# Two self-attentions: the product of exponentials and inverse sums is split by rows between VectorE and Pool

## What is computed

```
# third block (no mask)                     # fifth block (causal, q and k rotated)
scores = einsum('bhqd,bhkd->bhqk', q, k) / sqrt(dh)
attn = softmax(scores, axis=-1)
ctx = einsum('bhqk,bhkd->bhqd', attn, v)
out = ctx.reshape(B, S, D) @ wo.T + bo
```

## Time and profile before

| what | value |
|---|---|
| median of 3 runs | 3099.32 us (3094.27 to 3100.01) |
| the profiled execution | 3100.76 us, its span 3098.9 us |
| mean granted TensorE clock | 0.956 |
| busy share of the span | PE 92%, DVE 42%, ACT 31%, POOL 9% |
| stage 3's attention, scores to last output copy | 1026.4 to 1069.3 us of the span |
| stage 5's attention, scores to last output copy | 2855.5 to 2892.7 us of the span |

### The profile page before, as it was taken

The page is one execution under the profiler, slowest core; times in us unless marked ns, Lnnn a source line. Parts: engine busy times, 40 slices in busy tenths (PEclk is TensorE's granted clock), DMA queues, the critical chain, the costliest instruction groups (busy, mean ns, idle before and its releaser), DMA issues.

```text
span 3098.9 us, 36175 instructions
## 1 busy us (share of the span) xinstructions
PE 2852.6 (92%) x15608; PEld 1977.8 (64%) x15608; DVE 1305.4 (42%) x1978; ACT 973.3 (31%) x1471; POOL 263.6 (9%) x271
## 2 busy tenths in 40 slices
PE   7877989888898889999999969999999999997798
PEld 3335447356584468888888848878877877853432
DVE  4355374467731433333333342443343344354511
ACT  3233223124440344343334412332332332331300
POOL 1110110112000000000000011011001101000000
PEclk9988999998899989999999979999999999998799
DMA  8872794961021032222222210100100100012098
GB/s 354 314 280 97 303 375 164 359 236 65 14 82 68 30 111 102 99 95 95 96 95 95 97 70 21 45 21 25 45 25 21 45 25 21 25 62 95 29 414 358
DMA packets 63487, 385.23 MB, mean 124 GB/s; under 512 B 6193, under 2 KB 12593, under 8 KB 33889
## 3 DMA queue, kind: packets, MB, share of 16 engines
q1 hardware_dynamic: 27072, 190.58, 16.4%
q0 software_dynamic: 29776, 188.15, 15.8%
q10 hardware_dynamic: 6480, 4.20, 0.4%
HBM read 377.64 MB, written 5.26 MB: 124 GB/s over the span
## 4 chain that ended last, share of the span: by engine, by line
PE 76%; DVE 9%; DMA 7%; ACT 5%; issue 2%; POOL 1%; SPq 0%; DVEq 0%; POOLq 0%; ACTq 0%
PE PS L427 10%; PE PS L429 10%; PE PS L428 10%; PE PS L306 4%; PE PS L1707 4%; PE PS L614 4%; PE PS L1688 3%; PE PS L1671 3%; PE PS L1689 3%; PE PS L1690 3%; PE PS L1673 3%; PE PS L1672 3%; DMA ring<-in_experts 3%; PE PS L587 3%; PE PS L1724 2%; DMA PR<-in_ctxN 2%
## 5 line engine op out<-in xcount | busy, mean ns | idle before, releaser
L427 PE MATMUL PS<-X_high,W_high 128*128 128x512 f32 x576 | 226.4, 393 | 11.0 <-DVE X_low L1160 11.0
L427 PE MATMUL PS<-H_high,W_high 128*128 128x512 f32 x576 | 224.9, 390 | 2.1 <-DVE rstd L1461 2.1
L428 PE MATMUL PS<-X_low,W_high 128*128 128x512 f32 x576 | 225.8, 392 | 0.0
L429 PE MATMUL PS<-X_high,W_part 128*128 128x512 f32 x576 | 225.7, 392 | 0.0
L1107 DVE TENSOR_TENSOR W_part<-ring,W_high 128x2048 fp32r<-128x2048 f32 x63 | 147.0, 2334 | 185.0 <-ACT W_high L1103 185.0
L429 PE MATMUL PS<-H_high,W_part 128*128 128x512 f32 x576 | 224.7, 390 | 0.0
L428 PE MATMUL PS<-H_low,W_high 128*128 128x512 f32 x576 | 224.7, 390 | 0.0
L1103 ACT ACTIVATE W_high<-ring 128x2048 fp32r<-128x2048 f32 x72 | 137.0, 1915 | 252.4 <-PE PS L429 252.4
L1871 DVE TENSOR_TENSOR RB<-PS,rows 128x512 f32<-128x512 f32 x104 | 71.9, 691 | 306.8 <-PE PS L1690 306.8
L1146 DVE TENSOR_TENSOR H_low<-T,H_high 128x512 fp32r<-128x512 f32 x144 | 99.4, 690 | 210.5 <-ACT H_high L1133 210.4
L1671 PE MATMUL PS<-C_high,W_part 128*128 128x384 f32 (+2 forms) x512 | 177.3, 346 | 4.9 <-DVE W_part L1843 4.9
(11 more groups left out here) (336 smaller groups left out, 5571.8 us busy)
## 6 DMA issues: line engine op xcount, KB each, us to landing
ring<-in_experts SPq DMA_DIRECT2D x96, 1024.0 KB, 4.9
ring<-in_tiles SPq DMA_DIRECT2D x39, 1024.0 KB, 4.9
RC<-in_ctxN POOLq DMA_DIRECT2D x24, 1536.0 KB, 11.7
RA<-in_ctxT POOLq DMA_DIRECT2D x20, 1536.0 KB, 7.1
T<-in_ctxN POOLq DMA_DIRECT2D x24, 1024.0 KB, 14.3
RA<-in_experts SPq DMA_DIRECT2D x24, 1024.0 KB, 12.6
RA<-in_ctxT POOLq DMA_DIRECT2D x12, 1666.0 KB, 13.4
RB<-in_ctxT POOLq DMA_DIRECT2D x12, 1666.0 KB, 16.7
```

Source lines behind the costliest of these rows:

```text
L427: pe.matmul(ps, a, xh, start=start, stop=False)
L428: pe.matmul(ps, a, xl, start=False, stop=False)
L429: return pe.matmul(ps, b, xh, start=False, stop=stop)
```

## The change

Block bp's product for the rows 64 to 127 (u = 1) goes from DVE to Pool. DVE keeps the one for the rows 0 to 63 (u = 0). The shape, the operands and the output of each instruction stay as they are. Pool waits for its own instructions before, for DVE's reciprocal (which now has a name, `inverse{bp}`), and for the transposes of block bp - 2 or the zeros. PE's transposes wait for both products, and so does DVE's maxima(bp + 2), since it writes the `raw5` that both have read.

```diff
+        def attn_products(eng, at, tag, bp, u):
+
+            x, sm, r = raw5[bp % 2], sums[bp % 2], slice(u * S, (u + 1) * S)
+            if bp >= 2:
+                eng.wait_ge(*at.done(f"{tag}.T{bp - 2}.3"))
+            else:
+                eng.wait_ge(*at.done(f"{tag}.zero{bp}"))
+            eng.tensor_tensor(probs[bp % 2][r, :, r], x[r, :, :], sm[r, :].unsqueeze(2).broadcast_to([S, H, S]), ALU.mult).then_inc(*at.step(f"{tag}.p{bp}.{u}"))
...
+        def attn_pool_products(pool, at, tag):
+            for bp in range(NBP):
+                pool.wait_ge(*at.own())
+                pool.wait_ge(*at.done(f"{tag}.inverse{bp}"))
+                attn_products(pool, at, tag, bp, 1)
...
-                    pe.wait_ge(*at.done(f"{tag}.p{bp}"))
+                    for u in (0, 1):
+                        pe.wait_ge(*at.done(f"{tag}.p{bp}.{u}"))
...
                 if bp >= 2:
-                    dve.wait_ge(*at.done(f"{tag}.p{bp - 2}"))
+                    for u in (0, 1):
+                        dve.wait_ge(*at.done(f"{tag}.p{bp - 2}.{u}"))
...
-                dve.reciprocal(sm, sm).then_inc(*at.step())
+                dve.reciprocal(sm, sm).then_inc(*at.step(f"{tag}.inverse{bp}"))
                 dve.wait_ge(*at.own())
-                if bp >= 2:
-                    dve.wait_ge(*at.done(f"{tag}.T{bp - 2}.3"))
-                else:
-                    dve.wait_ge(*at.done(f"{tag}.zero{bp}"))
-                for u in (0, 1):
-                    r = slice(u * S, (u + 1) * S)
-                    dve.tensor_tensor(probs[bp % 2][r, :, r], x[r, :, :], sm[r, :].unsqueeze(2).broadcast_to([S, H, S]), ALU.mult).then_inc(*at.step(f"{tag}.p{bp}"))
+                attn_products(dve, at, tag, bp, 0)
...
             attn_pool(pool, at, "s3.at")
+            attn_pool_products(pool, at, "s3.at")
             expert_low(pool, at, MOE(0), 0)
...
             attn_pool(pool, at, "s5.at")
+            attn_pool_products(pool, at, "s5.at")
```

## The result

The changed kernel takes 3102.29 us (median of 22 runs) beside 3096.93 us of the kernel before (22 runs); the ratio is 1.0017, with a 95% interval of 1.0009 to 1.0024. That is 5.4 us more (2.8 to 7.4 by the interval), a small loss. Forecast were 5.2 us more, a range of 3098.5 to 3112 and 0.52 for "no change that can be told". By the forecast's own bound of 0.2% it is no change, and by its interval it is a loss. The forecast's 3104.5 lies 2.2 above the measured median because it was counted from the first three runs of the kernel before, whose median (3099.32) was 2.4 higher than that of all 22.

What follows compares the result with a forecast made beforehand. The prediction took DVE's chain through the attentions as the bound. Longer waits for Pool's half added 2.7 us in stage 3 and 2.5 in stage 5, so 3099.3 + 5.2 = 3104.5 us, range 3098.5 to 3112.

Steps and rivals of the forecast that it cites:

- What bounds it: Both attentions: DVE's chain sets the pace; maxima(2), maxima(3) and block 2's transposes wait for both halves, 0.90 each in stage 3.
- Turns instead of side by side: Product halves on DVE and Pool, two SBUF inputs each, exclude each other; only 0.14 to 0.15 us of the second's start hidden.
- DVE first: Behind each reciprocal DVE's half starts ahead of Pool's (lead of 0.24 us in earlier rows) and ends at +1.25.
- Pool's time: Pool's half of the product, 1024 elements a row: 2.35 us by a straight line through two earlier Pool operations.
- The step to who waits: From the end of Pool's half to the start of whoever waits for it: 0.05 us, giving +3.51 behind the reciprocal.
- PE's cover of block 3: Block 3's pair, ready at +7.0 in stage 3, lies hidden behind PE's T and O of block 2, until +8.22.
- rival 5: TensorE clock: T of block 2 at 2.4 GHz gives +3.0, 3102.3; a stretch more at 1.2 GHz costs 1.5. Chance 0.09.
- The sum: Added waits in both attentions: +2.7 us in stage 3 and +2.5 in stage 5, together +5.2 us.
- Pool dearer (1): Pool's product dearer through repeated input and gaps: at 3.5 us, +12.2, 3111.5; at 4.7 us, +21. Chance 0.12.
- Pool first (2): Pool gets its turn first, so block 2's out(1) and the sum wait for DVE's product: +7.5, 3106.8. Chance 0.08.
- Side by side (3): Product halves run side by side, Pool's ending at +2.50: -0.5 us, 3098.8. Chance 0.09.
- Faster (4): Product halves side by side, Pool at its one-input rate of 0.92 us: -3.9 and -4.1, 3091.3. Chance 0.02.

Runs made afterwards that it cites:

- the version with four buffers: Changed kernel with four buffers for the exponentials and the sums instead of two, so DVE's maxima no longer wait for Pool's half: 3094.05 us, 0.9985 against the kernel before.
- the run with PSUM: Changed kernel, but DVE's half reads its inverse sums from PSUM and the transposes use two PSUM banks instead of three: 3094.01 us, 0.9996 against the kernel before.
- Pool alone first: Changed kernel, but DVE's half waits for Pool's half of the same block: one run, 3108.4 us beside 3091.94 of the kernel before.
- the best version: Changed kernel with DVE's inverse sums in PSUM, four buffers, and block 3's scores ahead of block 0's output matmuls: 3089.69 us, 0.9982 against the kernel before.
- the two controls: Kernel before with transposes on two PSUM banks alone, 0.9999; kernel before with block 3's scores ahead of block 0's output matmuls alone, 1.0000.

## Why the prediction came out as it did

- **What bounds it: right.** The path goes through DVE, and the waits that cost are the three named: maxima(2), maxima(3), transposes of block 2. Removing the two buffer waits alone took the sum from +4.3 to -1.0 us. Of these 5.4 us, 4.1 came ahead of block 2's transposes; 1.3 came behind them, where PE ran at a higher clock.
- **Turns instead of side by side: right, and shown.** Same product, same shape: 2.88 us on Pool beside a two-SBUF-input half on DVE, 1.90 us with DVE idle, 1.90 us beside a half that reads PSUM. The second in turn hides 1.12 + 1.90 - 2.88 = 0.14 us of its start, the value read from the earlier trace rows. What "SBUF — State Buffer" of the Trainium skill states in "Who interferes with whom" holds here, its condition on DVE's second SBUF input included.
- **DVE first: right.** By 0.10 us instead of 0.24; what counts is the sign.
- **Pool's time: the term that was mis-sized.** "So 1024 elements take ... 2.35 us" measured 1.90. The line through the earlier trace rows is right for plain inputs (2.34 measured), and the repeated input costs 0.44 us less. Of the bounds I had expected the dearer side to be the open one.
- **The step to who waits: 0.05 assumed, 0.10 (PE) and 0.13 (DVE) measured.** I took it from a DVE-to-PE step; Pool's own is longer. Together with the line above a wait grows by 0.54 to 0.58 us instead of 0.90 to 0.96. Over six waits that is 2.2 us too much in my sum: up to the transposes of block 2, 1.64 us in either stage where I had 2.76.
- **PE's cover of block 3: right in kind, 1.35 us too cheap.** Block 3's pair is indeed hidden: Pool's half ends at 1064.92, and PE takes the transposes at 1067.20. But I let T and O of block 2 take the 4.67 and 4.48 us of before; they took 5.51 and 5.21. From start to start, T of block 3 came 5.44 and 5.14 us behind T of block 2, where the sum had 4.71 and 4.52. The windows over T (the first row) and O (the second) of stage 3's block 2, after:

```profile
1061.70:1065.30 3.60, 3.54 (x16) 3.27 (x16) 1.42 (x2) 1.79 (x3) 2.88 (x1) 0.50 0.00 0
1065.30:1067.20 1.90, 1.90 (x34) 1.39 (x33) 0.00 (x0) 0.60 (x1) 0.00 (x0) 0.50 0.00 0
```

  T and O both ran at 0.50, that is 1.2 GHz, and O took 1.94 us. Before, O took 1.18 us, in this window:

```profile
1064.00:1065.30 1.30, 1.24 (x33) 0.77 (x32) 1.25 (x2) 0.60 (x1) 0.00 (x0) 0.95 0.00 0
```

  In stage 5 O took 1.63 instead of 1.18. This is the other side of rival 5, which I had priced at 1.5 us a stretch; it cost 0.7 and 0.6. Why the clock stayed low isn't shown. Ahead of T, PE had stood idle for 3.40 us instead of 2.84, but the idle time alone does not decide: the version with four buffers had as much of it, and O at 1.18 us in both stages. Its stage 3:

```profile
1053.10 3.60 PE L1329 MATMUL PS<-sq,RC 128*128 128x128 f32 x16 [3.39 <-DVE misc L1382]
1056.64 1.18 PE L1338 MATMUL PS<-RC,T 128*32 128x128 f32 x32
```

- **The sum.** 5.2 forecast, less 2.24 for Pool's time and the steps, plus 1.35 for T and O at the lower clock, gives the +4.34 that the attentions measured; the profiled span has +4.0, the medians +5.4. The mechanism was right, but that the total came so close is in part luck: two errors of opposite sign cancelled by more than half. The 1.0 between attentions and medians is within the interval.
- **The rivals.** Pool dearer (1): no, cheaper. Pool first (2): no. Side by side (3): not as the change has it; the run with PSUM shows the halves so, and at a sum of -1.6 us, with Pool at 1.90 instead of 2.35 and one bank less. Faster (4): no.

## What to carry to other kernels

When both halves of an elementwise step have two SBUF inputs, giving one to Pool is a loss in itself: here they took turns, and Pool's rate (1.90 us for what DVE does in 1.22) replaced DVE's. Before splitting, see whether one of DVE's inputs can stand in PSUM (here for a copy of 0.17 us a block, and a bank that cost 0.7 us in all), and look which buffer reuse makes DVE wait for Pool: here those two waits cost more than the wait of PE. And work taken off an engine moves the end only up to the next thing that the engine waits for; find that one in the timeline (here the scores, 2.09 us) and move it as well.

## What was unexpected on the chip

- A second input repeated over 64 elements makes a two-input product on Pool cheaper, 1.90 instead of 2.34 us for 64 rows of 1024. DVE shows nothing like it: 1.22 us for the product, and 1.22 us for stage 5's mask addition (L1352, 1024 elements a row), whose second input isn't repeated element by element.
- Executions of one kernel differ ahead of the change's stage by more than the change's whole effect. Block 0's reciprocal of stage 3 ends between 1032.65 us (the four-buffer version with the scores moved) and 1047.19 us (inverse sums in PSUM and four buffers), although all that stands ahead of it is the same. From there to the span's end the profiles follow the sums, to within 2.4 us: before 2054.5 us, changed 2059.0, Pool alone first 2059.5, four buffers 2051.9, the best version 2047.8, the two controls 2054.5 and 2053.8. What causes the difference ahead of it stays open, and it wasn't tried. It would account for the intervals of 5 us on medians of 11 or more runs, and it is why the four-buffer version's 0.9985 shouldn't be read as 4.6 us of gain in the attentions, where it has 1.0.
